# Graph attention and experts on one core: the stage ahead of the experts taken in pairs of groups

## The reference, cut to what matters

```python
h0 = _gat_conv(x, W0, as0, ad0, b0, row, col)           # softmax over the incoming edges of a node
h1 = _gat_conv(x, W1, as1, ad1, b1, row[col], col[col]) # with loops
out = concatenate([h0, h1], -1) + x                     # x: the layer-normed input
x = x_in + layernorm(out) * gamma + beta
xf = layernorm(x)
gate_logits = xf @ Wg + bg
top_w, top_i = top_k(gate_logits, 2); top_w = softmax(top_w)
for e in range(8):                                      # only the two experts chosen count
    h = gelu(xf @ W1[e] + b1[e])
    out = out + w_dense[:, e:e + 1] * (h @ W2[e] + b2[e])
return x + out
```

## Time and profile before

| | |
|---|---|
| median of 3 runs | 3044.18 us (3039.81 to 3046.14) |
| profiled execution | 3036.07 us, span 3034.2 us |
| granted TensorE clock, mean | 0.831 |
| busy share of the span | PE 70%, DVE 72%, ACT 54%, POOL 62% |
| the stage's part that is read here | 2051 to 2275 us |
| experts | 2297 to 3034 us |

### The profile page before, as it was taken

The page is one execution under the profiler, slowest core; times in us unless marked ns, Lnnn a source line. Parts: engine busy times, 40 slices in busy tenths (PEclk is TensorE's granted clock), DMA queues, the critical chain, the costliest instruction groups (busy, mean ns, idle before and its releaser), DMA issues.

```text
span 3034.2 us, 42972 instructions
## 1 busy us (share of the span) xinstructions
PE 2131.5 (70%) x11674; PEld 2015.1 (66%) x11675; DVE 2188.6 (72%) x4468; ACT 1630.6 (54%) x2613; POOL 1885.4 (62%) x1868
## 2 busy tenths in 40 slices
PE   4600002788887887888888888703449999999998
PEld 2400002787887787887878887603438999999997
DVE  7678877788887787888888887788864444444443
ACT  5424423687777776877777777624433333333332
POOL 5777767777777777777777777777771222222222
PEclk8855555898999898989998998855559999999999
DMA  9446993444444444444444444565772222222222
GB/s 357 135 145 179 159 239 123 127 127 143 147 128 127 140 150 127 127 152 139 128 127 147 143 127 127 167 218 168 260 257 37 38 37 37 38 38 37 38 37 31
DMA packets 278910, 395.04 MB, mean 130 GB/s; under 512 B 156236, under 2 KB 231569, under 8 KB 272257
## 3 DMA queue, kind: packets, MB, share of 16 engines
q1 hardware_dynamic: 202945, 244.92, 25.4%
q0 software_dynamic: 74000, 145.58, 20.9%
q10 hardware_dynamic: 1840, 3.06, 0.3%
HBM read 201.61 MB, written 191.79 MB: 130 GB/s over the span
## 4 chain that ended last, share of the span: by engine, by line
POOL 45%; PE 26%; issue 15%; DVE 7%; DMA 3%; ACT 2%; DVEq 2%; SPq 0%; POOLq 0%; ACTq 0%
POOL AR L935 43%; PE ps L1453 12%; PE ps L1459 12%; POOL placed L1003 1%; PE ps L1329 1%; DMA tables<-AR 1%; DVE group_stats L2020 1%; ACT AR L1262 1%; DVE AR L1718 1%; DVE AR L1765 1%; DMA state<-AR 1%; POOL AR L967 0%; DVEq L1760 0%; POOL room L974 0%; DVE AR L2144 0%
## 5 line engine op out<-in xcount | busy, mean ns | idle before, releaser
L935 POOL DMA_INDIRECT AR<-tables,idx x1391 | 1326.3, 954 | 425.6 <-issue 423.2
L1358 PE MATMUL ps<-table_parts,onehot 128*128 128x408 f32 (+1 forms) x5848 | 1202.1, 371 | 300.8 <-DVE AR L1845 161.2
L1358 PEld LDWEIGHTS ps<-table_parts,onehot 128*128 128x128 f32 x5848 | 1166.1, 209 | 336.9 <-DVE AR L1845 175.4
L1143 ACT COPY AR<-AR 128x1984 f32<-128x1984 f32 (+3 forms) x110 | 401.4, 3649 | 328.9 <-DVE AR L1765 286.2
L1012 POOL DMA_INDIRECT out<-AR,idb x105 | 184.0, 1753 | 568.5 <-issue 537.6
L1765 DVE TENSOR_TENSOR_SCAN AR<-ps,AR 128x512 f32<-128x512 f32 x404 | 454.2, 1196 | 0.0
L1453 PEld LDWEIGHTS ps<-AR 128*128 128x128 f32 x3360 | 393.0, 193 | 31.9 <-issue 26.6
L1453 PE MATMUL ps<-AR 128*128 128x128 f32 x3360 | 393.6, 276 | 26.5 <-DVE AR L2238 26.5
L1758 DVE TENSOR_TENSOR AR<-AR,ps 128x3968 f32<-128x3968 f32 (+1 forms) x51 | 356.6, 6991 | 0.0
L2238 DVE COPY AR<-AR 128x1024 f32 x210 | 151.1, 720 | 207.4 <-PE ps L1453 205.6
L1218 ACT ACTIVATE onehot<-onehot 128x1536 fp32r<-128x1536 f32 (+1 forms) x172 | 269.4, 1566 | 5.5
(11 more groups left out here) (345 smaller groups left out, 2456.7 us busy)
## 6 DMA issues: line engine op xcount, KB each, us to landing
state<-AR SPq DMA_DIRECT2D x50, 2232.0 KB
AR<-tables,idx POOLq DMA_INDIRECT x1440
AR<-in_L_ffn_W SPq DMA_DIRECT2D x16, 1024.0 KB
AR<-placed SPq DMA_DIRECT2D x420, 32.0 KB
AR<-adstart SPq DMA_DIRECT2D x50, 248.0 KB, 4.0
adstart<-room SPq DMA_DIRECT2D x21, 496.0 KB, 14.0
tables<-AR SPq DMA_DIRECT2D x49, 136.0 KB, 2.4
room<-tables SPq DMA_DIRECT2D x14, 476.0 KB, 4.2
```

Of the source, the lines that this page charges most:

```text
L935: pool.indirect_dma_start(out=G[s][:, j, 0:ROWT], out_offset=None, in_=table_rows, in_offset=bass.IndirectOffsetOnAxis(ap=idx[:, s, j:j + ...
L1143: return S.copy(to.rearrange("p j (h c) -> p j h c", h=HD)[:, :, :, a:z], of[:, :, 1:n + 1].rearrange("p (c h) j -> p j h c", h=HD)[:, :, ...
L1358: return T.matmul(bank[:, 0:z], mark, table_parts[:, k, v * w:v * w + z], start=(a == 0 and k == 0), stop=(a == LEV - 1 and k == PARTS - 1))
```

## The change

The stage takes its groups in units: (0, 1), (2, 3), (4, 5) and (6). For the second convolution the units are (0, 1), (2, 3), (4) and (5, 6).

- `shares` and the small part of `combine` (now `weights`) run once per unit, on 128 x 112 elements where a unit has two groups. The large part of `combine` stays per group.
- `layer_stats` takes 14 tiles: one reciprocal, one shift, one root on ScalarE.
- `choose(u)` and `settle(u)` take 14 tiles: 14 MAX, 14 MAX_INDEX, and each other instruction once. `ranks(u)` on TensorE has 16 products in place of 9.
- `choose(u-1)` stands in the first statistics of unit u, ahead of the reciprocal that releases ScalarE; `settle(u-1)` stands between the two `conclude`s of unit u.
- GpSimd gathers the states of all 7 groups first, and places a unit (28 scatters) when its `ipos` is there.
- On VectorE the repair of boundary rows (`fix_sums(2)`) now comes ahead of `shares(1, 1)`, after two `combine`s as before; SyncE waits for two groups before it stores the first.

```diff
-OWN_ORDER = ((1, 0), (1, 1), (1, 2), (1, 3), (1, 4), (0, 0), (0, 1), (0, 2), (1, 5), (0, 3), (1, 6), (0, 4), (0, 5), (0, 6))
+UNITS = ((0, 1), (2, 3), (4, 5), (6,))
+UNITS2 = ((0, 1), (2, 3), (4,), (5, 6))
+NU = len(UNITS)
+UT = 2 * GRP
+OWN_ORDER = ((1, 0), (1, 1), (1, 2), (1, 3), (1, 4), (0, 0), (0, 1), (1, 5), (1, 6), (0, 2), (0, 3), (0, 4), (0, 5), (0, 6))
...
# SyncE
+                for u, unit in enumerate(UNITS):
+                    for g in unit:
+                        rows_ahead(g)
+                    for g in unit:
+                        store_rows(g)
+                    for e in ((), (1,), (2, 3), (4, 5))[u]:
+                        down_in(e)
...
# GpSimd
             for n in range(2):
                 last_states1(n)
             last_states2(5, 2, GRP)
-            for n in range(2, 4):
+            last_states2(6)
+            for n in range(2, NG):
                 last_states1(n)
-            last_states2(6)
...
-            for n in range(NG):
-                place(n)
-                if n + 4 < NG:
-                    last_states1(n + 4)
+            for u, unit in enumerate(UNITS):
+                pool.wait_ge(places_ready, u + 1)
+                for i, n in enumerate(unit):
+                    for k in range(2):
+                        for t in range(GRP):
+                            at = i * GRP + t
+                            pool.indirect_dma_start(out=placed, out_offset=bass.IndirectOffsetOnAxis(ap=ipos[:, u % 2, k, at:at + 1], axis=0),
+                                                    in_=pr[n % 4][:, t, :], in_offset=None).then_inc(tokens_placed[n % 4], 16)
...
# ScalarE
+            for u, unit in enumerate(UNITS):
+                deviations(u, 0)
+                if u == 0:
+                    share_exps(1, 3)
+                else:
+                    gate_exp(u - 1)
+                act.wait_ge(group_scales_ready, 2 * u + 1)
+                for i, g in enumerate(unit):
+                    for t in range(GRP):
+                        at = i * GRP + t
+                        last = S.activation(halves[g][:, t, :], halves[g][:, t, :], ACT.Identity, bias=group_scale[:, 2, at:at + 1], scale=group_scale[:, 1, at:at + 1])
+                    last.then_inc(group_normalised, 1)
+                deviations(u, 1)
+                if u + 1 < NU:
+                    share_exps(0, u + 1)
+                act.wait_ge(group_scales_ready, 2 * u + 2)
+                for i, g in enumerate(unit):
+                    rows_normalised(g, i * GRP)
+            gate_exp(NU - 1)
...
# VectorE
             shares(0, 0)
-            for g in range(NG):
-                combine(0, g)
-
-                def next_shares():
-                    if g + 1 < NG:
-                        shares(0, g + 1)
-                    if 2 <= g <= 3:
-                        shares(1, 3 + g)
-
-                layer_stats(halves[g], g, 0, next_shares)
-                if g >= 1:
-                    choose(g - 1)
-                if 2 <= g <= 3:
-                    combine(1, 3 + g)
-                conclude(g)
-            choose(NG - 1)
-            settle(NG - 1)
+            for u, unit in enumerate(UNITS):
+                weights(0, u)
+                for g in unit:
+                    combine(0, g)
+
+                def while_first_deviates():
+                    if u == 0:
+                        shares(1, 3)
+                    else:
+                        choose(u - 1)
+
+                layer_stats([halves[g] for g in unit], u, 0, while_first_deviates)
+                conclude(unit[0])
+                if u >= 1:
+                    settle(u - 1)
+                for g in unit[1:]:
+                    conclude(g)
+
+                def while_second_deviates():
+                    if u + 1 < NU:
+                        shares(0, u + 1)
+
+                layer_stats([X[:, g * GRP:(g + 1) * GRP, :] for g in unit], u, 1, while_second_deviates)
+                if u == 0:
+                    weights(1, 3)
+                    for g in UNITS2[3]:
+                        combine(1, g)
+            choose(NU - 1)
+            settle(NU - 1)
```

More of the change, by code:

```diff
@@ L1440, in _ @@
                     if t >= 2:
-                        logits(g, t - 2)
-                logits(g, GRP - 1).then_inc(logits_ready, 1)
-            ranks(NG - 1)
-            pe.wait_ge(masks_then_sum_ready, NG + 1)
-            T.matmul(ps[6][:, GRP * NEX:GRP * NEX + NEX], ones[:, :], mask_sum[:, NG, :], start=True, stop=True).then_inc(ranks_then_totals_ready, 1)
+                        logits(g, first, t - 2)
+                return logits(g, first, GRP - 1)
+            for u, unit in enumerate(UNITS):
+                if u >= 1:
+                    ranks(u - 1)
+                for i, g in enumerate(unit):
+                    mm = turn_rows(g, i * GRP)
+                mm.then_inc(logits_ready, 1)
+            ranks(NU - 1)
+            pe.wait_ge(masks_then_sum_ready, NU + 1)
+            T.matmul(ps[6][:, GRP * NEX:GRP * NEX + NEX], ones[:, :], mask_sum[:, NU, :], start=True, stop=True).then_inc(ranks_then_totals_ready, 1)
             def up(s, t):
@@ new lines, in layer_stats, with state_views @@
+                meanwhile()
+                dve.wait_ge(deviations_ready, NG + 2 * u + q + 1)
+                V.reciprocal(group_scale[:, 1, 0:n], group_scale[:, 0, 0:n])
+                dd()
+                V.scalar_tensor_tensor(group_scale[:, 2, 0:n], group_mv[:, 0:n, 0], -1.0, group_scale[:, 1, 0:n], ALU.mult, ALU.mult).then_inc(group_scales_ready, 1)
+            def state_views(k, unit):
+                where = (states1, states2)[k]
+                if len(unit) == 2 and (k == 0 or unit[0] == 0):
+                    a = unit[0] % 4
+                    flat = AR[:, states1_at + a * GRP * ROWS:states1_at + (a + 2) * GRP * ROWS] if k == 0 else eb2f[:, 0:2 * GRP * ROWS]
+                    return [(0, UT, flat.rearrange("p (t r) -> p t r", r=ROWS))]
+                return [(i * GRP, (i + 1) * GRP, where[g % 4]) for i, g in enumerate(unit)]
@@ L2043, in shares @@
+            def shares(k, u):
+                unit = (UNITS, UNITS2)[k][u]
+                n = GRP * len(unit)
+                z = share_of[:, k, :, 0:n, :]
+                gt = slice(unit[0] * GRP, unit[0] * GRP + n)
+                for g in unit:
+                    dve.wait_ge((states1_gathered, states2_gathered)[k][g % 4], 16 * GRP * (g // 4 + 1))
                 zk = own_score[:, gt, k * HD:(k + 1) * HD]
-                V.tensor_tensor(z[:, 0], sg[:, :, ROWT:ROWS], bc(bare[:, k, gt].unsqueeze(2), [P, GRP, HD]), ALU.add)
+                for a, e, sg in state_views(k, unit):
+                    V.tensor_tensor(z[:, 0, a:e, :], sg[:, :, ROWT:ROWS], bc(bare[:, k, unit[0] * GRP + a:unit[0] * GRP + e].unsqueeze(2), [P, e - a, HD]), ALU.add)
@@ L2135, in settle @@
+                V.tensor_copy(ipos[:, u % 2, :, 0:n], pos[:, :, 0:n]).then_inc(places_ready, 1)
                 dd()
```

246 lines of the change are left out of this document (114 added, 132 removed).

## The result

| | before | changed |
|---|---|---|
| median, 7 runs each on one chip | 3042.45 us (3039.73 to 3046.14) | 3053.43 us (3050.03 to 3054.81) |
| profiled execution | 3036.07 us, span 3034.2 | 3050.61 us, span 3048.8 |
| VectorE busy | 2188.6 us | 2171.6 us |

The ratio is 1.0035, 95% interval 1.0025 to 1.0045: the change costs 11.0 us. The forecast was 3060.6 (3051 to 3070) and slower; sign and range held, the range near its low end, and the cost came out a third smaller than the 16.4 us of the sum.

The account below looks back on a forecast made before the run. GpSimd's scatters, by when they are released, bound the stage: start T0 2059 plus a 232.5 us chain ends at 2291.5 against 2275.06, +16.4 us; 3044.18 + 16.4 = 3060.6 us, range 3051 to 3070.

Parts of the forecast that it names:

- Prices of 14 tiles: VectorE's predicted times for two-group instructions: weights 2.1 us, shares with scale 1.45, settle 2.4, statistics 6.2, choose 4.95.
- Rival 3: The 14-tile forms on VectorE save nothing, adding 17 us up to the third places, 3078 us; chance 0.07.
- The waits: VectorE waits 3.7 us for ScalarE in each unit and about 9 us for TensorE's logits ahead of the third choose.
- I take 1 us of waiting: In unit 0, VectorE's shares(0, 1) was taken to wait 1 us for the gathers of groups 2 and 3.
- From group 3 on it doesn't even wait: In the kernel before, GpSimd was read as bound by its scatters from group 3 on, without waiting for ipos.
- VectorE's saving of 18.5 us: Three pairs save VectorE 17 us, and the pair (5, 6) of the second convolution 1.4.
- rival 1: VectorE decides: its saving of 18.5 us less 8 for the late start gives -10.5 us, 3033.7; chance 0.06.
- T0: Start of the stage, the first share, waiting for group 1's gathers: 2059, 8 us later than before; bounds 2056 to 2061.7.
- 8.1 us above that execution: Distance of the median before (3044.18) from its profiled execution (3036.07), carried over to the changed kernel's forecast.
- I count nothing: Padding rows, issued by SyncE, were expected to end about 1.5 us before the last scatters land, so cost nothing.
- Rival 2: Scatters stay hidden: GpSimd has unit 2 placed by 203.3, end +4.8 us, 3049; needs 0.84 us a scatter; chance 0.06.
- Lengthened scatters: GpSimd's scatters slowed beside VectorE: some 4 us in the first block, none in the last 42, at most 4.4 more.

Follow-up runs that it names:

- e6: The kernel before, with only the first share of the first convolution also waiting for the gathers of group 1; ratio 1.0018 against before.
- e9: The kernel before, with only the early repair of maxima and sums, ahead of shares(1, 2) and behind combine(1, 1) alone; ratio 0.9992 against before.
- e7: The changed kernel with units (0,1), (2,3), (4), (5), (6) and choose(u-1) behind the reciprocal and shift that release ScalarE; ratio 1.0011 against before.
- e1: The kernel before, with only GpSimd reordered: all gathers first, then scatters in blocks of 28, 28, 28 and 14, ipos in four buffers; ratio 1.0062 against before.
- e8: The changed kernel with first-convolution groups single, GpSimd's order as before, choose(u-1) behind the first statistics' reciprocal and shift; second convolution still in pairs; ratio 0.9982 against before.
- e4: The changed kernel with choose(u-1) and its exponential moved behind the reciprocal and shift that release ScalarE; ratio 1.0027 against before.

## Why the prediction was right, and what was off

Its claim was that the releases of scatters decide, not VectorE's work. Step by step, in us from the first share:

| step | predicted | measured |
|---|---|---|
| first block of scatters starts | 86.4 | 85.8 |
| second block | 133.2 | 132.0 |
| third block | 179.8 | 178.5 |
| idle ahead of second and third block | 7, 8 | 7.2, 7.4 |
| from third release to the end | 52.7 | 52.8 |
| end of the last scatter | 232.5 | 231.3 |
| first share against before | +8 | +4.2 |
| end of the last scatter against before | +16.4 | +11.5 |

None of the three signs of being wrong appeared: the third block began at 2235.16 and not before 2222, the last 14 scatters did not wait for `ipos`, and the first share moved.

- **Prices of 14 tiles.** Weights 2.1 against 2.17, choose 4.95 against 4.98, settle 2.4 against 2.34 held; statistics 6.2 came out at 5.9. Rival 3 (nothing saved, 3078) is out.
- **The waits** for ScalarE (3.7 against 3.61) and for TensorE's logits (9 against 9.43) held. "I take 1 us of waiting" ahead of `shares(0, 1)` failed; the row has no wait:

```profile
2096.22 0.28 DVE L2078 TENSOR_TENSOR room<-AR,bare 128x112 f32<-128x112 f32 x1
```

With the shorter statistics that covers the 1.2 us by which the chain was sooner.
- **Readings that were wrong.** "From group 3 on it doesn't even wait" holds for groups 3 and 4 only. Group 6 waits 2.59 us, and group 5 2.03:

```profile
2237.67 0.96 POOL L1003 DMA_INDIRECT placed<-AR,ipos  x1 [2.03 <-DVE ipos L2134]
```

So near the end VectorE's release bound the kernel before too, and e6's 7.6 us fit that. VectorE's saving of 18.5 us was too high: by the prediction's own prices shares save 0.9 a pair and not 1.2, and the busy time, which leaves gaps out, fell by 13.8. Its arrivals in units 2 and 3 (115.9 and 154.7) sum to 115.4 and 153.9 by its own terms. The forecast's sum uses none of these, since the logits come later; rival 1 does.
- **T0 is the mis-sized term.** "The last gather starts at 2053 to 2054" was nearly right (2053.99, which by the boundary gather is 2052.63 on the clock of before), "lands by 2059" was not. I took 5.6 us of landing from group 0's gather; it took 2.65 (2053.99 to 2056.64). That gather is issued after SyncE's transfers have ended. Busy share of the DMA engines in tenths, and GB/s, in 40 slices: of the changed kernel, 2040 to 2060, then of the kernel before, 2035 to 2060.

```profile
DMA  8999999999999999998999999980230602205032
GB/s 373 416 430 430 397 438 386 428 375 418 366 443 394 385 426 400 425 382 256 346 315 315 325 309 300 368 221 0 65 83 0 148 0 74 74 0 147 0 74 74
```
```profile
DMA  0040437999999999999999998999140400500225
GB/s 0 0 118 0 118 31 192 339 422 417 424 390 429 424 390 439 402 389 459 374 386 428 401 428 290 364 295 337 43 118 0 118 0 0 118 0 0 52 66 84
```

The engines are full until 2053.5 in the one and until 2052.5 in the other. The gather of before is issued at 2045.45, inside; that of the changed kernel at 2053.99, behind. e6 and e9, both with VectorE's groups as before, show the same: e6's gather of 2057.62 lands in 2.63, and e9's of 2047.04 in 6.51. Over the twelve traces such a gather takes 5.5 to 6.5 us issued amid those transfers and 2.6 at their end or behind; e7's, issued some 2 us ahead of their end, takes 2.99. This was in the trace of before to be read, and is 3 of the 4.9 us.

- **The total.** The sum said 3052.5 for a profiled execution; it is 3050.61: 4.9 less by T0 and the chain, 1.4 more ahead of the boundary gather, and 1.7 more behind the last scatter. The remaining 5.3 us of the 7.2 by which 3060.6 missed the median are the step "8.1 us above that execution". 1.7 of them are the median before, 3044.18 of 3 runs and 3042.45 of 7; the other 3.6 are that this median stands 6.4 above its profiled execution and the changed kernel's only 2.8. One profiled execution says little about that distance.
- **Behind the last scatter** the first product of the experts comes 8.6 us after the end of the last scatter, 8.0 before, and the first answer another 15.4 us later, 14.3 before, with a granted clock of 0.82 in that stretch against 0.88. Ahead of the first product TensorE had been idle for 38.9 us, before for 26.5. Why the clock was lower was not tested. The 0.6 and the 1.1 us are the 1.7. "I count nothing" for the padding rows stands near its edge. SyncE's waits in the changed kernel (line, what was waited for, us in total, times, longest):

```profile
SPq L837 <- DMA placed<-padrow: 5.7, 1, 5.7
SPq L838 <- DMA placed<-AR,ipos: 0.8, 1, 0.8
```

SyncE waits 5.7 us for the padding rows and only 0.8 more for the scatters (3.5 and 4.5 before): had the scatters ended 1 us sooner, the padding rows would be the bound. That the 0.6 us are theirs was not tested.

- **Rival 1**, VectorE decides, is refuted by the change itself (13.8 us less busy, 11.0 slower) and by e1 (VectorE's instructions unchanged, +17.3). **Rival 2**, hidden scatters, by 52.79 us for 42.
- **Lengthened scatters.** The last 42, without VectorE's large instructions beside them, follow every 1.26 us and are 0.96 long. The 28 of the first block take 39.0 (2142.44 to 2188.64 - 7.20 = 2181.44), 3.6 more than 28 x 1.263; its first lasts 2.30, beside the gamma products of 2141.86, and those beside the statistics 0.96. The Trainium skill (SBUF — State Buffer, Who interferes with whom) says that a VectorE instruction with two inputs in SBUF contends with a GpSimd one that reads SBUF, for a port pair that is an exclusive lock. The trace agrees: 2.30 beside such products, 0.96 beside statistics, which have one input. All 8 scatters of the changed kernel that last over 1.1 us overlap a large two-input instruction of VectorE. But not every overlap lengthens: the scatter of 2159.49 takes 0.96 beside the addition of 2159.59 (L2125).
- The Trainium skill (Perfetto Trace Analysis, Optimizing Scalar/DVE Operations) has larger operations for a saturated engine and smaller ones where others have bubbles. The runs agree with its second half: the last scatter of e8, with the smaller units, ends 17.8 us sooner than the changed kernel's.

## What to carry to other kernels

Where one engine hands work to a queue with a fixed price per item, compute the end as last release + items still behind it x price; merging groups saves instructions on the producer but doubles what stands behind each release and delays the first. Shares of busy time can't show this: here the producer got 13.8 us cheaper and the kernel 11.0 us slower. e8 keeps the merging where no one waits for the parts (the second convolution's pairs), and releases the consumer ahead of the producer's next statistics, one group at a time. It beats both kernels, though no run separates these two.

## What the runs showed of the hardware

- An indirect gather of 128 rows landed in 2.63 (e6) and 2.65 us (changed) when it was issued behind the direct transfers, and in 5.5 to 6.5 us when it was issued amid them, at about 400 GB/s.
- A scatter of 128 rows costs GpSimd 1.26 to 1.27 us from start to start, in every kernel here, over runs of 14 to 42. One alone is busy for 0.96 us, and for up to 2.81 (e4) beside VectorE's two-input products.
- On VectorE 14 tiles' statistics take 4.67 us where 7 take 2.38: one instruction per tile gains nothing from a pair. A product on 112 elements takes 0.27 to 0.28 us where 56 take 0.22, and a reciprocal 0.85 (2058.95 in the changed kernel) where 56 take 0.50.
